# Softmax-free linear attention over 16 images: denominators by column halves, one reciprocal a group, and other orders in the last batch

## The chip, the cores and the metric

The kernel runs on one core of a Trainium2 chip. The metric is the device time of one execution in microseconds (us), lower is better. A core has TensorE (PE, its weight loads shown apart as PEld), VectorE (DVE), ScalarE (ACT), GpSimd (POOL) and SyncE (SP, which here issues every DMA). Each engine works through its own instructions in order; semaphores tie the engines together. A difference of about 0.2% is what a measurement of this kernel can tell from no change.

## What is computed

For each of 16 images x[b] of 256 channels by 6400 tokens (80 by 80), the layer normalises in groups of 8 channels, makes q, k and v, and forms linear attention with 8 heads of 32 channels:

```
xt = gn(x).reshape(B, C, N).transpose(0, 2, 1)
q, k, v = split(xt @ qkv_w.T + qkv_b)            # N = 6400, C = 256
q = relu(q);  k = relu(k + pos_enc)
z = 1 / (einsum('bic,bc->bi', q, k.sum(axis=1)) + 1e-6)   # per head and token
kv = einsum('bjc,bjd->bcd', k, v)                # 32 x 32 per head
out = einsum('bic,bcd,bi->bid', q, kv, z)
y = x + (out @ proj_w.T + proj_b).transpose(0, 2, 1)
```

The change touches z, the reciprocals of the denominators, and how the last image is finished. Everything is float32 at the edges.

## The kernel before

**Tiles.** An image is 13 blocks of tokens: t = 0 to 11 of 512 tokens and t = 12 (LAST) of 256. A block of all 256 channels is a tile of 128 partitions by 2 by 512 (512 KB). B = 16 batches n are one image each, and a batch has 13 steps, one for each block.

**The pipeline.** At step t of batch n, TensorE transposes block t, makes its keys (L603), adds them to the Gram matrix (L615, L617), makes queries for block t-2 (L627), and makes the output of block t-3 of the batch before (L663, 12 matmuls for a block of 512). The Gram matrix and the key sum of batch n-1 are complete only when batch n starts, so the small work that closes batch n-1 lies in the first steps of batch n. We call it the junction: key sums, `key_scale`, `kv_product`, the denominators of group 0 (blocks 0 to 7) at the end of step 0, `m_product` at step 1, and the denominators of group 1 (blocks 8 to 12) at step 2.

**Denominators** (L648). The stationary operand is a window of 32 columns of `swin`, in which the key sums of one half of the channels stand in the columns of four heads and the rest is zero. Each matmul writes 32 partitions of one PSUM bank; four matmuls with j = 0 to 3 write the four strips of 32 partitions. In a strip, half the 32 rows (16 of them) are used, and each row holds 512 tokens. ScalarE adds 1e-6 and copies the bank to `zt` (`z_plus`, L1154). VectorE inverts it in two instructions of 256 columns (`invert`, L937), for group 0 both at step 1, for group 1 one at step 3 and one at step 4. SyncE writes it to HBM (`store_z`, L415, and four small ones for the tail, L420) and then reads it back for each block, copied to the 32 partitions of each head (`load_zb`, L433). GpSimd multiplies q by it (`scale`, L1338).

**Who waits for whom.** In each step VectorE's `key_low` (L885) follows the `invert` of step 1; ScalarE's `key_keep` (L1119) waits for `key_low`, and `normalise` (L1090) stands behind it; SyncE's next load of `xa` (L348) waits for `normalise`, and `store_z` stands behind that load in SyncE's queue. GpSimd takes `scale`, `key_sum` (L1315), `xn_low` (L1301) and `u_low` (L1342) in this order, and TensorE's next key matmuls (L603) need `xn_low`.

**The end** (`finish`, from step 12 of batch 15 on). There is no next batch to work beside, so the outputs of blocks 9 to 12 of batch 14 and of all 13 blocks of batch 15 stand in a row on TensorE. For each block of batch 15, SyncE loads z (`load_z_last`, L433), GpSimd multiplies (`scale_last`, L1331), ScalarE copies twice (`u_last`, L1250 and L1261), VectorE subtracts (`u_low`, L998), TensorE makes the output, and VectorE adds x to it (`residual`, L899). The x of the last batch is loaded once more (`load_last`, L359) into seven places for 512 tokens, used in turn: blocks 4 to 6 wait for a store of batch 14, and blocks 7 to 11 wait for the store of block t-7 of batch 15 (`y_last`). All of it goes through SyncE's one queue.

The order on each engine is the order in which the functions below issue it; nothing reorders it.

## Time and profile before

| | us |
|---|---|
| median of 3 runs | 2628.76 |
| lowest, highest | 2627.99, 2630.11 |
| the profiled execution, its own time | 2629.6 |
| its span, first to last instruction | 2627.5 |
| TensorE busy in it | 2568.3 |
| granted TensorE clock, mean | 0.999 |

The span and what lies around it (2.1 us) make up the profiled execution's time. TensorE is busy for 98% of the span, so its idle stretches, the stretch before it starts and the one after it ends are where time can be won or lost; busy time of another engine counts only where TensorE or the last store waits for it.

### The profile page before, as it was taken

What the parts mean: (1) busy time and instruction counts of PE and PEld (TensorE: products, weight loads), DVE (VectorE), ACT (ScalarE), POOL (GpSimd) and SP (SyncE); (2) the same over time, 40 slices, a digit from 0 to 9 for tenths busy, and PEclk for the clock granted to TensorE, in tenths of its full rate; (3) what the DMA queues carried; (4) which work ended last, traced back from release to release, by engine and by line L of the source; (5) the groups of instructions that cost most, each with busy time, mean ns of one, the idle gap of its engine ahead of it and who ended that gap; (6) DMA issues with size and microseconds to landing.
All of it is one profiled execution on the core that took longest, in us unless ns stands there. A gap on an engine that the chain in (4) does not pass through costs nothing.

```text
span 2627.5 us, 45059 instructions
## 1 busy us (share of the span) xinstructions
PE 2568.3 (98%) x15940; PEld 2203.1 (84%) x15940; DVE 1515.9 (58%) x2405; ACT 1698.8 (65%) x2705; POOL 1979.7 (75%) x1234
## 2 busy tenths in 40 slices
PE   4999999999999999999999999999999999999998
PEld 3878888888888888888888888888888888888886
DVE  5656555565555556555555555656555555554547
ACT  4766766666666666766667666666666666666654
POOL 4958778687787778868687786887768778687875
PEclk9999999999999999999999999999999999999999
DMA  7547867677776867767777677786867677676658
GB/s 257 191 159 254 271 223 264 233 259 254 239 268 225 274 227 260 260 238 256 234 268 261 225 262 251 248 272 222 264 236 263 234 255 258 234 247 205 229 197 300
DMA packets 324189, 642.15 MB, mean 244 GB/s; under 512 B 25728, under 2 KB 47104, under 8 KB 323968
## 3 DMA queue, kind: packets, MB, share of 16 engines
q1 hardware_dynamic: 323968, 639.28, 72.6%
q8 instruction: 130, 2.13, 0.3%
q14 instruction: 91, 0.75, 0.1%
HBM read 519.25 MB, written 119.93 MB: 243 GB/s over the span
## 4 chain that ended last, share of the span: by engine, by line
PE 91%; issue 2%; DVE 2%; POOL 2%; DMA 2%; ACT 1%; SPq 0%; DVEq 0%; ACTq 0%; POOLq 0%
PE banks L603 21%; PE banks L627 20%; PE banks L663 19%; PE banks L615 13%; PE banks L617 7%; PE banks L594 6%; PE banks L648 3%; DMA q<-in_x 1%; PE banks L678 1%; DVE zt L937 1%; POOL hl L1301 0%; POOL kacc L1315 0%; DMA y<-xr 0%; PE banks L685 0%; POOL posb L1326 0%
## 5 line engine op out<-in xcount | busy, mean ns | idle before, releaser
L1315 POOL TENSOR_TENSOR kacc<-kacc,kt 128x512 f32<-128x512 f32 x368 | 477.7, 1298 | 277.3 <-ACT kt L1119 275.5
L1301 POOL TENSOR_TENSOR hl<-xn,hl 128x512 fp32r<-128x512 f32 x384 | 488.9, 1296 | 217.6 <-ACT hl L1102 217.5
L603 PE MATMUL banks<-wqk,hl 128*128 128x256 f32 x4608 | 645.0, 289 | 7.3 <-POOL hl L1301 7.3
L869 DVE TENSOR_TENSOR xt<-banks,xt 128x512 fp32r<-128x512 f32 x400 | 274.9, 687 | 590.0 <-ACT xt L1107 589.7
L627 PE MATMUL banks<-hl,wqk 128*128 128x512 f32 x2304 | 600.0, 396 | 0.2 <-ACT zt L1154 0.2
L615 PE MATMUL banks<-kk,xt 128*128 128x512 f32 x1600 | 583.8, 399 | 3.3 <-DVE kk L885 3.3
L603 PEld LDWEIGHTS banks<-wqk,hl 128*128 128x128 f32 x4608 | 575.0, 191 | 9.1 <-POOL hl L1301 9.1
L663 PE MATMUL banks<-uhl,mhl 128*128 128x512 f32 (+1 forms) x2316 | 541.8, 383 | 2.1 <-DVE xr L899 2.1
L663 PEld LDWEIGHTS banks<-uhl,mhl 128*128 128x128 f32 x2316 | 423.6, 188 | 89.9 <-issue 2.5
L1338 POOL TENSOR_TENSOR q<-q,zb 128x1024 f32<-128x1024 f32 x180 | 433.8, 2410 | 74.5 <-DMA zb<-z_rows 74.4
L627 PEld LDWEIGHTS banks<-hl,wqk 128*128 128x128 f32 x2304 | 406.7, 188 | 92.0 <-issue 1.3
L1112 ACT ACTIVATE kk<-banks 128x512 fp32r<-128x512 f32 x400 | 238.9, 597 | 357.8 <-DVE banks L880 356.0
L617 PE MATMUL banks<-kk,xt 128*128 128x256 f32 x1600 | 449.2, 281 | 0.0
L1342 POOL TENSOR_TENSOR uhl<-q,uhl 128x1024 fp32r<-128x1024 f32 x178 | 427.4, 2401 | 7.2 <-ACT uhl L1136 7.2
L899 DVE SCALAR_TENSOR_TENSOR xr<-banks,biases,xr 128x512 f32<-128x512 f32 x368 | 274.3, 750 | 249.7 <-PE banks L663 247.9
L885 DVE SCALAR_TENSOR_TENSOR kk<-banks,kk 128x512 fp32r<-128x512 f32 x400 | 273.5, 684 | 190.1 <-ACT kk L1112 187.7
L1119 ACT ACTIVATE kt<-banks 128x512 f32<-128x512 f32 x400 | 238.6, 596 | 222.7 <-DVE kk L885 222.6
L1131 ACT ACTIVATE q<-banks,biases 128x512 f32<-128x512 f32 x382 | 262.1, 686 | 147.0 <-PE banks L627 145.3
L615 PEld LDWEIGHTS banks<-kk,xt 128*128 128x128 f32 x1600 | 302.2, 189 | 60.0 <-issue 4.0
L617 PEld LDWEIGHTS banks<-kk,xt 128*128 128x128 f32 x1600 | 303.4, 190 | 0.0
L880 DVE TENSOR_TENSOR banks<-banks,posb 128x512 f32<-128x512 f32 x400 | 276.3, 691 | 12.4 <-PE banks L603 11.4
L1090 ACT ACTIVATE xn<-xa,nbias,rstd 128x512 f32<-128x512 f32 x360 | 272.9, 811 | 0.0
(120 smaller groups left out, 2341.5 us busy)
## 6 DMA issues: line engine op xcount, KB each, us to landing
posb<-pos_plus_bk SPq DMA_DIRECT2D x375, 256.0 KB, 5.0
xs<-in_x SPq DMA_DIRECT2D x184, 512.0 KB, 6.9
xa<-in_x SPq DMA_DIRECT2D x184, 512.0 KB, 6.0
xr<-in_x SPq DMA_DIRECT2D x184, 512.0 KB, 3.9
zb<-z_rows SPq DMA_DIRECT2D x184, 512.0 KB, 6.0
y<-xr SPq DMA_DIRECT2D x184, 512.0 KB, 7.0
z_rows<-zt SPq DMA_DIRECT2D x32, 256.0 KB, 5.5
xr<-in_pos SPq DMA_DIRECT2D x25, 256.0 KB, 4.7
```

Source lines behind the costliest of these rows:

```text
L603: last = mm(psK[:, par(n, h), i * C:(i + 1) * C], hl_of(t)[:, a, c, s:s + P], wqk[:, w, c, C:2 * C], start=(j == 0), stop=(j == len(terms) ...
L615: mm(psG[:, c, :], xt[:, hp, 0, i, c * P:(c + 1) * P], kk[:, hp, i, :, :], start=(h == 0 and i == 0), stop=False)
L617: last = mm(psG[:, c, C:2 * C], xt[:, hp, 1, i, c * P:(c + 1) * P], kk[:, hp, i, 0, :], start=False, stop=(h == NHB - 1 and i == TILES - 1))
L627: last = mm(dst, wqk[:, w, c, m * P:(m + 1) * P], hl_of(t)[:, a, c, :], start=(j == 0), stop=(j == len(terms) - 1))
L663: last = mm(dst, mw[:, w, c, m * P:(m + 1) * P], u[:, a, c, 0:k], start=(j == 0), stop=(j == len(terms) - 1))
L869: v.tensor_tensor(xt[:, hp, 1, :, :].rearrange("p i n -> p (i n)"), psT, xt[:, hp, 0, :, :].rearrange("p i n -> p (i n)"), ALU.subtract).t ...
L880: v.tensor_tensor(psK[:, par(n, h), :], psK[:, par(n, h), :], posb[:, s, :], ALU.add).then_inc(kt_ready, 1)
L899: v.scalar_tensor_tensor(out=xs_, in0=src, scalar=pb[:, m:m + 1], in1=xs_, op0=ALU.add, op1=ALU.add).then_inc(out_ready, 1)
L1301: g.tensor_tensor(hl_of(t)[:, 1, :, s], xn_of(n, t)[:, :, s], hl_of(t)[:, 0, :, s], ALU.subtract).then_inc(xl_ready, 1)
L1315: g.tensor_tensor(both, both, kt[:, par(n, h), :], ALU.add).then_inc(ks_done, 1)
L1338: g.tensor_tensor(q_of(n, t), q_of(n, t), zb_of(t), ALU.mult).then_inc(u_ready, 1)
L1342: g.tensor_tensor(u[:, 1, :, 0:size(t)], q_of(n, t), u[:, 0, :, 0:size(t)], ALU.subtract).then_inc(ul_ready, 1)
```

## The change

The denominators are laid out in another way. Each matmul of 512 columns becomes two of 256, for the first and the second half f of the block, written to neighbouring rows; all 32 rows of a strip are then used, and the bank is 256 columns wide instead of 512. `zt`, the rows in HBM, the copy on ScalarE and the reciprocal shrink to 256 columns with them, and one reciprocal stands for two. For the tail block (f = 0 alone) the four matmuls of 64 columns for each half of the channels stay, now all writing columns 0 to 63 of their strips. Group 1 is inverted at step 3 as a whole; in batch 1 (n == 1) the reciprocal of group 0 moves behind `key_low`.

In `finish`, x of the last batch gets a place of its own for each block (free slots of `q` among them), so blocks 4, 5 and 9 to 11 wait for a `u_low` and blocks 6 to 8 for a store of batch 14, none for a store of its own batch. SyncE's queue is put in another order, `u_low(0)` goes ahead of `m_low` on VectorE, the left-over copies of batch 14 go earlier on ScalarE and GpSimd, and `m_total` leaves its sum in the PSUM bank instead of `mt`; the second `u_last` therefore waits for `ml_ready`.

```diff
@@ constants and buffers @@
-WIN = 12
+WIN = 20
-        zt = sb("zt", [P, 2, BLK])
+        zt = sb("zt", [P, 2, HALF])
-        zd = nc.dram_tensor("z_rows", (2, P, BLK), F32, kind="Internal").ap()
+        zd = nc.dram_tensor("z_rows", (2, P, HALF), F32, kind="Internal").ap()
@@ last_of, load_last @@
-            return (xs[:, 0], xs[:, 1], xa[:, 0], xa[:, 1], xr[:, 0], xr[:, 1], xr[:, 2])[t % 7]
+            return (xs[:, 0], xs[:, 1], xa[:, 0], xa[:, 1], q_of(B - 2, LAST - 2), q_of(B - 2, LAST - 1),
+                    xr[:, 0], xr[:, 1], xr[:, 2], q_of(B - 1, 0), q_of(B - 1, 1), q_of(B - 1, 2))[t]
-                s = last_slot(t)
-                if t in (4, 5, 6):
-                    sp.wait_ge(y_stored[t - 4], landed3(B - 2, t + 5))
-                elif 7 <= t < LAST:
-                    sp.wait_ge(y_last[s], last_no(t) - 16)
-                sp.dma_start(last_of(t), x_part(B - 1, t)).then_inc(x_last[s], 16)
+                if t in (4, 5):
+                    sp.wait_ge(ul_ready, blk_no(B - 2, t + 6))
+                elif t in (6, 7, 8):
+                    sp.wait_ge(y_stored[t - 6], landed3(B - 2, t + 3))
+                elif t in (9, 10, 11):
+                    sp.wait_ge(ul_ready, blk_no(B - 1, t - 9))
+                sp.dma_start(last_of(t), x_part(B - 1, t)).then_inc(x_last[t], 16)
@@ denominators (tensor) @@
-                        w = WIN - 8 * s - c
-                        for j in range(4):
-                            t = 8 * g + 4 * s + j
-                            if g == 1 and s == 1:
-
-                                cols = slice(j * HALF // 4, (j + 1) * HALF // 4)
-                                data = q_of(n, LAST)[:, c, cols]
-                            else:
-                                cols = slice(0, BLK)
-                                data = q_of(n, t)[:, c, :]
-                            last = mm(bank[32 * j:32 * j + 32, cols], swin[:, c, w:w + 32], data,
-                                      start=(s == 0 and c == 0), stop=(s == 1 and c == CC - 1))
+                        for f in range(2):
+
+                            w = WIN - 16 * s - 2 * c - f
+                            for j in range(4):
+                                t = 8 * g + 4 * s + j
+                                if g == 1 and s == 1:
+
+                                    if f == 1:
+                                        continue
+                                    k = HALF // 4
+                                    cols, data = slice(0, k), q_of(n, LAST)[:, c, j * k:(j + 1) * k]
+                                else:
+                                    cols, data = slice(0, HALF), q_of(n, t)[:, c, f * HALF:(f + 1) * HALF]
+                                last = mm(bank[32 * j:32 * j + 32, cols], swin[:, c, w:w + 32], data,
+                                          start=(s == 0 and c == 0 and f == 0), stop=(s == 1 and c == CC - 1 and f == 1 - g))
@@ invert, step, finish (vector) @@
-            def invert(n, g, parts=(0, 1)):
+            def invert(n, g):
                 dve.wait_ge(zt_ready, 2 * n + g + 1)
-                for i in parts:
-                    v.reciprocal(zt[:, g, i * HALF:(i + 1) * HALF], zt[:, g, i * HALF:(i + 1) * HALF]).then_inc(rc_ready, 1)
+                v.reciprocal(zt[:, g, :], zt[:, g, :]).then_inc(rc_ready, 1)
-                if t == 1 and junction:
+                if t == 1 and n > 1:
                     invert(n - 1, 0)
+                if t == 1 and n == 1:
+
+                    invert(n - 1, 0)
-                if t in (3, 4) and junction:
-                    invert(n - 1, 1, (t - 3,))
+                if t == 3 and junction:
+                    invert(n - 1, 1)
@@ z_plus, finish (scalar) @@
-                a(zt[:, g, :], bank, ACT.Identity, bias=zeps).then_inc(zt_ready, 1)
+                if g == 1:
+                    wait(act, z_tail_stored, 64 * n)
+                a(zt[:, g, :], bank[:, 0:HALF], ACT.Identity, bias=zeps).then_inc(zt_ready, 1)
-                        act.wait_ge(m_sum, n)
+                        act.wait_ge(ml_ready, n)
+                u_left(q2, hl[:, 0], q_done, two_no(n - 1, 8, 1))
                 save_q(n - 1, q2, 1, 0)
                 save_q(n - 1, q1, 0, 2)
+                u_left(q1, hl[:, 1], q_done, two_no(n - 1, 9, 1))
                 z_plus(n - 1, 0, psK[:, 0, :])
-                u_left(q2, hl[:, 0], q_done, two_no(n - 1, 8, 1))
-                u_left(q1, hl[:, 1], q_done, two_no(n - 1, 9, 1))
+                u_left(q0, uhl, o_done, two_no(n - 2, q2 - 1, 1))
                 z_plus(n - 1, 1, psK[:, 1, :])
-                u_left(q0, uhl, o_done, two_no(n - 2, q2 - 1, 1))
+                u_last(0)
                 m_high_last()
-                for t in range(NBLK):
+                for t in range(1, NBLK):
@@ end (gpsimd) @@
-            for t in (LAST - 1, LAST):
-                scale(B - 2, t)
-            for t, u in ((LAST - 2, hl[:, 0]), (LAST - 1, hl[:, 1]), (LAST, uhl)):
-                u_low(B - 2, t, u)
+            scale(B - 2, LAST - 1)
+            u_low(B - 2, LAST - 2, hl[:, 0])
+            scale(B - 2, LAST)
+            u_low(B - 2, LAST - 1, hl[:, 1])
+            u_low(B - 2, LAST, uhl)
```

What this makes of the queues at the three places in question is shown below, as the programs issue it. Line numbers of the changed program are one to five off.

VectorE at the junction of batch 1, step 1: `x_low_t` (xt), `key_add` (banks), the reciprocals of group 0 (zt), `key_low` (kk). Before:

```order
L880 TENSOR_TENSOR banks<-banks,posb 128x512 [waits k_done,pos_landed0]
L937 RECIPROCAL zt<-zt 128x256 [waits zt_ready]
L937 RECIPROCAL zt<-zt 128x256
L885 SCALAR_TENSOR_TENSOR kk<-banks,kk 128x2x256 [waits kh_ready]
L869 TENSOR_TENSOR xt<-banks,xt 128x512 [waits xth_ready]
```

Changed:

```order
L881 TENSOR_TENSOR banks<-banks,posb 128x512 [waits k_done,pos_landed0]
L886 SCALAR_TENSOR_TENSOR kk<-banks,kk 128x2x256 [waits kh_ready]
L937 RECIPROCAL zt<-zt 128x256 [waits zt_ready]
L870 TENSOR_TENSOR xt<-banks,xt 128x512 [waits xth_ready]
L881 TENSOR_TENSOR banks<-banks,posb 128x512 [waits k_done,pos_landed1]
```

One reciprocal is gone and the other has moved behind `key_low`; in batches 2 to 15 one is gone and the other keeps its place.

VectorE in `finish`, from the second reciprocal on; `mt` or `banks` at L925 and L926 is `m_total`, `hl_tail` is `m_low`, `hl` is `u_low(0)`, `xr` and `xr_tail` are the residuals of batch 14. Before:

```order
L937 RECIPROCAL zt<-zt 128x256 [waits zt_ready]
L899 SCALAR_TENSOR_TENSOR xr<-banks,biases,xr 128x512 [waits o_done,xr_landed1]
L899 SCALAR_TENSOR_TENSOR xr<-banks,biases,xr 128x512 [waits o_done]
L925 SCALAR_TENSOR_TENSOR mt<-bpb,ksc,banks 128x256 [waits m_done]
L925 SCALAR_TENSOR_TENSOR mt<-bpb,ksc,banks 128x256
L937 RECIPROCAL zt<-zt 128x256 [waits zt_ready]
L932 TENSOR_TENSOR hl_tail<-mt,hl_tail 128x512 [waits mh_ready]
L899 SCALAR_TENSOR_TENSOR xr<-banks,biases,xr 128x512 [waits o_done,xr_landed2]
L899 SCALAR_TENSOR_TENSOR xr<-banks,biases,xr 128x512 [waits o_done]
L998 TENSOR_TENSOR hl<-banks,hl 128x1024 [waits uh_ready]
```

Changed:

```order
L937 RECIPROCAL zt<-zt 128x256 [waits zt_ready]
L900 SCALAR_TENSOR_TENSOR xr<-banks,biases,xr 128x512 [waits o_done,xr_landed1]
L900 SCALAR_TENSOR_TENSOR xr<-banks,biases,xr 128x512 [waits o_done]
L926 SCALAR_TENSOR_TENSOR banks<-bpb,ksc,banks 128x256 [waits m_done]
L926 SCALAR_TENSOR_TENSOR banks<-bpb,ksc,banks 128x256
L1001 TENSOR_TENSOR hl<-banks,hl 128x1024 [waits uh_ready]
L933 TENSOR_TENSOR hl_tail<-banks,hl_tail 128x512 [waits mh_ready]
L900 SCALAR_TENSOR_TENSOR xr<-banks,biases,xr 128x512 [waits o_done,xr_landed2]
```

The last reciprocal is gone, and `u_low(0)` now stands ahead of `m_low` and of the residual of block 11.

SyncE in `finish`, from the last z load of the first five on; `xn`, `kt` and `zb` are the places of z, `xr` and `q` from `in_x` are x of the last batch, `y` is a store. Before:

```order
L374 DMA y<-xr 128x2x512 [waits out_ready]
L359 DMA xr<-in_x 128x2x512 [waits y_stored0]
L374 DMA y<-xr 128x2x512 [waits out_ready]
L415 DMA z_rows<-zt 128x512 [waits zb_tail_landed,rc_ready,zb_landed1,zb_landed0]
L420 DMA z_tail_rows<-zt 8x64 x4
L433 DMA xn<-z_rows 128x1x1024 [waits z_stored0,u_ready]
L374 DMA y<-xr 128x2x512 [waits out_ready]
L359 DMA xr<-in_x 128x2x512 [waits y_stored1]
L433 DMA xn<-z_rows 128x1x1024 [waits z_stored0,u_ready]
L374 DMA y<-xr_tail 128x2x256 [waits out_ready]
L433 DMA kt<-z_rows 128x1x1024 [waits z_stored0,u_ready]
```

Changed:

```order
L355 DMA q<-in_x 128x2x512 [waits ul_ready]
L370 DMA y<-xr 128x2x512 [waits out_ready]
L411 DMA z_rows<-zt 128x256 [waits zb_tail_landed,rc_ready,zb_landed1,zb_landed0]
L416 DMA z_tail_rows<-zt 16x64 x4
L355 DMA xr<-in_x 128x2x512 [waits y_stored0]
L370 DMA y<-xr 128x2x512 [waits out_ready]
L429 DMA xn<-z_rows 128x1x1024 [waits z_stored0,u_ready]
L355 DMA q<-in_x 128x2x512 [waits ul_ready]
L429 DMA xn<-z_rows 128x1x1024 [waits z_stored0,u_ready]
L370 DMA y<-xr 128x2x512 [waits out_ready]
L355 DMA xr<-in_x 128x2x512 [waits y_stored1]
L355 DMA q<-in_x 128x2x512 [waits ul_ready]
```

The store of group 1's rows has moved ahead of the first load that waits for a store of y. The z of block 7 (`kt`) still stands behind the second such load; two x loads into `q` have come between.

## Rows read from the trace of the kernel before

**Rows 1.** The page, part 1: busy us, share of the span, instructions.

```profile
PE 2568.3 (98%) x15940; PEld 2203.1 (84%) x15940; DVE 1515.9 (58%) x2405; ACT 1698.8 (65%) x2705; POOL 1979.7 (75%) x1234
```

**Rows 2.** Waits: engine, line, released by: us in total, times, longest us.

```profile
PE banks L603 <- POOL hl L1301: 7.3, 7, 2.0
```

**Rows 3.** Groups of instructions by form: shapes, count, busy us, mean ns.

```profile
L648 PE MATMUL banks<-q,swin 128*32 128x512 f32 x764 | 89.0, 596 | 0.0
...
L648 PE MATMUL banks<-q_tail,swin 128*32 128x64 f32 x256 | 6.5, 219 | 0.0
...
L937 DVE RECIPROCAL zt<-zt 128x256 f32<-128x256 f32 x64 | 109.4, 1730 | 6.6 <-ACT zt L1154 6.6
```

**Rows 4.** Timeline, PE: start us, us, line, count; denominators of one junction.

```profile
1128.49 3.64 PE L648 MATMUL banks<-q,swin 128*32 128x512 f32 x32
...
1156.38 0.41 PE L648 MATMUL banks<-q_tail,swin 128*32 128x64 f32 x16
```

**Rows 5.** Timeline, junction of batch 1, PE and DVE; brackets: idle before, its releaser.

```profile
180.07 0.47 PE L615 MATMUL banks<-kk,xt 128*128 128x512 f32 x1 [0.76 <-DVE kk L885]
...
184.53 0.63 PE L594 MATMUL banks<-ident,xn 128*128 128x128 f32 x4 [1.22 <-DVE xt L869]
...
176.03 3.35 DVE L937 RECIPROCAL zt<-zt 128x256 f32<-128x256 f32 x2
```

**Rows 6.** Chain that ended last: denominators of group 0 in three batches, start us, us.

```profile
1929.47 3.57 PE banks L648 x32
...
2089.34 3.57 PE banks L648 x32
...
2250.59 3.57 PE banks L648 x32
```

**Rows 7.** Timeline, POOL at two junctions, and SP at the second of them.

```profile
1473.47 2.40 POOL L1338 TENSOR_TENSOR q<-q,zb 128x1024 f32<-128x1024 f32 x1 [4.69 <-DMA zb<-z_rows]
...
2114.36 2.39 POOL L1338 TENSOR_TENSOR q<-q,zb 128x1024 f32<-128x1024 f32 x1 [6.27 <-DMA zb<-z_rows]
...
2103.14 0.40 SPq L415 DMA_DIRECT2D z_rows<-zt  x1
2108.45 0.52 SPq L433 DMA_DIRECT2D zb<-z_rows  x1
```

**Rows 8.** Timeline, PE at the end: outputs of blocks 11, 12, then batch 15.

```profile
2580.30 1.67 PE L663 MATMUL banks<-uhl,mhl 128*128 128x256 f32 x12 [2.12 <-DVE xr L899]
2582.00 5.74 PE L663 MATMUL banks<-hl,hl_tail 128*128 128x512 f32 x24
...
2601.53 3.00 PE L663 MATMUL banks<-uhl,hl_tail 128*128 128x512 f32 x12 [1.86 <-DVE xr L899]
...
2616.09 4.31 PE L663 MATMUL banks<-hl,hl_tail 128*128 128x512 f32 x24
```

**Rows 9.** Timeline, DVE: the last two residuals.

```profile
2620.05 1.41 DVE L899 SCALAR_TENSOR_TENSOR xr<-banks,biases,xr 128x512 f32<-128x512 f32 x2 [1.16 <-DMA xr<-in_x]
2621.38 0.86 DVE L899 SCALAR_TENSOR_TENSOR xs_tail<-banks,biases,xs_tail 128x256 f32<-128x256 f32 x2
```

**Rows 10.** Timeline, SP at the end: issues of stores and loads.

```profile
2567.11 0.34 SPq L415 DMA_DIRECT2D z_rows<-zt  x1
2569.24 1.17 SPq L433 DMA_DIRECT2D xn<-z_rows  x2
...
2572.40 0.62 SPq L374 DMA_DIRECT2D y<-xr  x1
2580.59 0.38 SPq L359 DMA_DIRECT2D xr<-in_x  x1
...
2584.84 0.52 SPq L433 DMA_DIRECT2D xn<-z_rows  x1
```

**Rows 11.** Windows: us, busy of PE, PEld, DVE, ACT, POOL, PEclk, DMA share, GB/s.

```profile
2560.00:2565.00 5.00, 5.00 (x40) 2.59 (x33) 1.34 (x1) 1.28 (x3) 0.75 (x1) 1.00 0.02 5
...
2605.00:2610.00 5.00, 4.97 (x22) 3.76 (x21) 3.92 (x6) 3.54 (x4) 4.14 (x2) 1.00 1.05 402
```

62 lines of the change are left out of this document (30 added, 32 removed).

## Prediction, made before the changed kernel ran

> **What bounds the kernel now.** I read the page's busy shares first. TensorE is busy for 98% of the span [rows 1], at the full granted clock; VectorE, for which most of this change is written, for 58%. So VectorE's saving cannot be the answer by itself: 32 reciprocals of 1.73 us [rows 3] are 55 us of VectorE, and what they are worth is what TensorE waits for behind them. Second, the waits of TensorE. Apart from the start, which the change leaves alone, they are few: seven waits for `xn_low` with 7.3 us in sum [rows 2], about half of it in the start, and some at the junction of batch 1 and after batch 15's last key block. Third, the timelines at those places, which give three stretches where TensorE or the last store is held up by something that this change touches. They are the three terms below. Everywhere else TensorE works through an unchanged list without a gap, 159.87 us from one junction's denominators to the next [rows 6].
>
> **The denominators on TensorE: 0.** Group 0 had 16 matmuls, each recorded twice, 32 records in 3.64 us [rows 4]. Now it has 32 matmuls of half the columns. Four strips run at once, and a set of four records of 512 columns takes (3.64 - 0.60) / 7 = 0.43 us, start to start. Halving the columns gives 0.21 us for twice as many sets: 15 x 0.217 + 0.38 = 3.64 us again, where 0.38 is a record of 256 columns by the line through 0.596 us at 512 and 0.219 us at 64 [rows 3]. The risk is a cost for each record that doesn't shrink. The records of 64 columns bound it: 16 of them take 0.41 us, so they start (0.41 - 0.22) / 15 = 13 ns apart [rows 4], and a record of 256 columns has 53 ns to hide such a step. I take 0. The upper bound is the part of a record that doesn't depend on its columns, 0.219 - 64 x 0.84 ns = 0.165 us, paid once more by each added set: 8 sets in group 0 and 4 in group 1, 12 x 16 batches x 0.165 = 32 us. The tail's matmuls keep count and size. A lower bound under zero has no source, since the columns streamed are the same.
>
> The Trainium skill, page TensorEngine Tiling (Array Packing), section Instruction Overhead, speaks against this split: each matmul carries about 60 cycles of overhead, so that very short ones cost as much as ones of 60 columns. At 2.4 GHz that would be an estimated 25 ns for each of the 768 added records, 19 us, and 2639 us in all. The trace's 13 ns between records of 64 columns doesn't agree with it where four strips run side by side.
>
> **ScalarE, DMA, GpSimd in the junctions: 0.** `z_plus` and the row stores get shorter, the reads for each block keep their 4 KB runs, and one more wait (`z_tail_stored`) is for stores of a batch ago. The SyncE queue keeps its order there.
>
> **Term 1, junction of batch 1: 2.0 us.** The two reciprocals take 3.35 us from 176.03, `key_low` stands behind them, and TensorE waits 0.76 us for it at 180.07. ScalarE's `normalise` and the next transposed copy are late for the same reason, and TensorE waits another 1.22 us at 184.53 [rows 5]. With `key_low` first, it comes 3.3 us earlier, and the single reciprocal of 1.73 us fits before VectorE's next work. Both waits go: 0.76 + 1.22 = 2.0. Next late is the `key_low` of step 2 behind statistics, a wait that exists now and stays. Bounds 0.8 (only the first goes) and 2.2.
>
> **Term 2, late z rows in three batches: 3.9 us.** In each junction SyncE issues the store of the rows (2103.14) only after an `xa` load that waits for `normalise`, which waits for `key_low`, which waits for the reciprocals. The read goes out at 2108.45 and GpSimd waits for it, with `xn_low` queued behind [rows 7]. In twelve of the fifteen junctions it waits 4.69 us at most and TensorE notices nothing. In three the read lands late, GpSimd waits over 6 us, 6.27 at the most, and the batch takes longer: 2089.34 to 2250.59 is 161.25 us against 159.87 [rows 6], 1.38 more. The other two give slightly less; I take 3.9 for the three. One reciprocal fewer makes `key_low`, the `xa` load and the row store 1.6 us earlier, so the wait of 6.27 becomes 4.7, in the class that costs nothing. I take all 3.9. Bounds: 0, if the landings get later by as much as the issues get earlier, and 4.1, since no other batch has anything to give. Group 1 has the same gain, a step earlier, and nobody waits there.
>
> **Term 3, the end: 3.5 us** (bounds 0 and 6.0), in three pieces.
>
> First, when the first output of batch 15 starts (2582.00 [rows 8]). One reciprocal of group 0 less lets the row store go at 2565.2 instead of 2567.11, and the first z reads at 2567.3 instead of 2569.24 [rows 10]. GpSimd, which had three `u_low` left, now has only that of block 12, which waits for TensorE's block 9 and is done before the read lands. So it scales block 0 from about 2571.5 to 2574, ScalarE copies twice (2 us), VectorE has `u_low(0)` at 2577.5, then `m_low` and the residual of block 11, for which TensorE waits 2.12 us now. That output starts near 2579, and block 0 at 2580.8: gain 1.2. Here a danger lies: `u_low(0)` now stands ahead of `m_low` and of the residual, so a z read that lands late delays TensorE's block 11/12 hand-over too. Bounds 0 and 1.4.
>
> Second, the run of 13 outputs. It takes from 2582.00 to 2620.40 = 38.4 us; 24 records take 5.74 us, so a block takes (5.74 - 0.40) / 23 x 12 = 2.78 us, and 12 blocks and a tail of half the columns 34.7. The 3.7 between are mostly waits for blocks whose z came late, 1.86 of them before 2601.53 [rows 8]. The z of block 5 was issued at 2584.84, behind the store of group 1's rows and an x load that waited for a store of y until 2580.59 [rows 10]. Now the row store goes out at 2574, ahead of that wait. The wait itself stays: the store it waits for goes out at about 2571 instead of 2572.40, with one more x load ahead of it, and lands near 2580. So z of block 5 is issued at 2581, of block 6 at 2582, in time. But the next x load waits for the store of block 10, issued at 2580.3, until 2588.3 (8 us, as 2572.40 to 2580.59 [rows 10]), and z of block 7 stands behind it, at 2589.5. It lands about 7 us later, and 6 us more of GpSimd, ScalarE and VectorE give 2602.6, where TensorE could take it at 2600.3. That gives 2.3 back. Gain 1.4; bounds -1 and 3.7.
>
> Third, the last residuals. VectorE waits 1.16 us for x of block 11, which pushes the tail's from 2620.4 to 2621.4 [rows 9]. With a place for every block, x is there: gain 0.9, bounds 0 and 0.9. The store of the last tile and its 5.2 us to the end stay.
>
> DMA is the cover for all of this. Its share is 0.02 in 2560 to 2565 and 1.05 from 2605 to 2610 [rows 11]. The bytes stay (but for 0.25 MB of rows), two x loads move into the idle time, and so the queue of transfers ends earlier; but in the middle it stays full.
>
> **Sum.** 2.0 + 3.9 + 3.5 = 9.4 us off the profiled execution's own 2629.6 gives 2620.2. That execution lies 0.8 us above the median of 2628.76; how many late landings the other runs had isn't shown, and since the forecast has none, I don't lower it: 2620.
>
> **Rivals.** (a) *The z rows stay late.* The read is issued 1.6 us earlier but lands in another mix of loads. Against it: the waits fall into those up to 4.69 and those over 6, nothing between. Then term 2 is zero: 2624.1. Chance 0.13. (b) *The end gives nothing.* The x loads wait for stores of batch 14 still, everything after is behind them, and the transfer queues are full there. Terms 1 and 2 alone: 2623.7. Chance 0.12. (c) *The end is free.* No late z at all, 6.0 instead of 3.5: 2617.7. Chance 0.09. (d) *The split matmuls cost TensorE time*, at each junction, on the engine that sets the pace. Between 13 ns for each of 768 added records (10 us) and 0.165 us for each added set (32 us) it gives 2630 to 2652; it decides from 9.4 us, that is 12 ns a record. For it: the smallest spacing seen is about that. Against it: that spacing is an eighth of the 107 ns between records of 512 columns, just as the columns are, so nothing in it is fixed. Chance 0.05, of which 0.04 end slower by more than 0.2%.
>
> **How the numbers follow.** The forecast has 0.59 and by itself the range 2617 to 2623. What is left over, 0.02, is slower by a mishap at the end. A difference of 0.2% (5.3 us) is about what a measurement of this kernel can tell from no change: faster is under 2623.5. The forecast and (c) give 0.68, half of (b) and a fifth of (a) add 0.09: 0.77. Within 0.2% is the rest of these and 0.01 of (d): 0.17. Slower 0.06. The range, 2616 to 2624.5, takes in (a), (b) and (c) and leaves out (d).
>
> **What would show it.** Right: denominators of group 0 again about 3.64 us for 64 records; no wait at 180 and 184; GpSimd's wait at the junctions 3 to 4.7 us and all batches 159.9 us apart; block 0's output near 2574.9 (2580.8 less the 5.9 of terms 1 and 2), one wait of some 2 us before block 7, and no wait of VectorE for x. Wrong: groups of denominators longer by 0.4 us or more, waits of over 6 us at junctions, or an end that is as long as now from block 0's output on (from 2582.00 to the span's 2627.5 now 45.5 us; forecast 2624.0 - 2580.8 = 43.2).

## The result and the profile after

| | before, us | changed, us |
|---|---|---|
| median | 2628.76 | 2620.66 |
| lowest, highest of 7 executions each | 2625.24, 2630.11 | 2618.88, 2622.67 |
| the profiled execution, its own time | 2629.6 | 2620.28 |
| its span | 2627.5 | 2618.5 |

The ratio of changed to before is 0.9971 [0.996, 0.9983]. Measured again beside other kernels it was 0.9974 [0.9964, 0.9984], with a median of 2621.09. The forecast was 2620.0, range 2616 to 2624.5. So the total came out as forecast, but two pieces of its third term did not: the run of outputs at the end got longer instead of shorter, and the last stores won more than they were given.

The page of the changed kernel, part 1, answers to [rows 1]:

```profile
PE 2569.6 (98%) x16708; PEld 2229.5 (85%) x16708; DVE 1470.2 (56%) x2373; ACT 1691.9 (65%) x2705; POOL 1979.4 (76%) x1234
```

VectorE lost 45.7 us of busy time and TensorE gained 1.3, yet the time fell by 8.1. Neither number is the answer; it lies where TensorE stood still. The groups by form, columns as in [rows 3]:

```profile
L649 PE MATMUL banks<-q,swin 128*32 128x256 f32 x1528 | 89.5, 381 | 0.0
...
L937 DVE RECIPROCAL zt<-zt 128x256 f32<-128x256 f32 x32 | 55.8, 1743 | 6.3 <-ACT zt L1158 6.3
```

Twice the records with half the columns have nearly the busy time of before (89.5 against 89.0), and 32 reciprocals are left of 64. The timeline of the junction of batch 1, TensorE and VectorE, against [rows 4, 5]:

```profile
169.73 3.66 PE L649 MATMUL banks<-q,swin 128*32 128x256 f32 x64
...
189.90 0.47 PE L614 MATMUL banks<-kk,xt 128*128 128x512 f32 x1 [0.56 <-DVE kk L886]
...
177.55 1.74 DVE L937 RECIPROCAL zt<-zt 128x256 f32<-128x256 f32 x1
```

The group of denominators takes 3.66 us, 0.02 more than before. The waits of 0.76 and 1.22 us are gone; the wait of 0.56 us at step 2 is the only bracket that TensorE shows between the two groups of denominators.

**Where the 9.0 us of span went.** The starts of group 0's denominators, read in both timelines, cut the span into the same stretches:

| stretch, us | before | changed | gain |
|---|---|---|---|
| start to the denominators of junction 1 | 169.66 | 169.73 | -0.07 |
| junction 1 to junction 2 | 159.50 | 157.15 | 2.35 |
| junctions 2 to 15, 13 batches | 2082.48 | 2078.78 | 3.70 |
| junction 15 to `finish` | 147.59 | 147.64 | -0.05 |
| denominators of `finish` to the end of the span | 68.27 | 65.20 | 3.07 |

In the third row all 13 batches of the changed kernel take 159.90 or 159.91 us. Before, nine took 159.86 or 159.87, one 160.07, and three 161.24, 161.26 and 161.11, of which the second is the one in [rows 6, 7]. GpSimd's waits for the rows of denominators in junctions 2 to 15, a line of the view of waits (in total, times, longest us), before and after:

```profile
POOL q L1338 <- DMA zb<-z_rows: 71.0, 18, 6.3
```

```profile
POOL q L1343 <- DMA zb<-z_rows: 66.8, 21, 5.4
```

The end of the changed kernel, timeline of TensorE, against [rows 8]; the first line is the output of block 12 of batch 14, then come blocks of batch 15:

```profile
2573.00 1.67 PE L664 MATMUL banks<-uhl,mhl 128*128 128x256 f32 x12 [0.68 <-DVE xr L900]
2574.51 5.63 PE L664 MATMUL banks<-hl,hl_tail 128*128 128x512 f32 x24
...
2591.94 2.98 PE L664 MATMUL banks<-uhl,hl_tail 128*128 128x512 f32 x12 [0.65 <-DVE q L900]
2597.16 7.32 PE L664 MATMUL banks<-hl,hl_tail 128*128 128x512 f32 x24 [2.23 <-DVE q L900]
2604.99 2.98 PE L664 MATMUL banks<-xt,hl_tail 128*128 128x512 f32 x12 [0.52 <-DVE xr L900]
...
2610.53 4.31 PE L664 MATMUL banks<-hl,hl_tail 128*128 128x512 f32 x24
```

The wait of 2.12 us ahead of block 12's output is 0.68 us now. The run of 13 outputs goes from 2574.51 to 2614.84: 40.3 us, where it took 38.4. It waits 0.65, 2.23 and 0.52 us, and the group at 2597.16 (blocks 7 and 8) takes 7.32 us instead of some 5.6, as at 2604.37 in the trace of before. The windows of that stretch (us, busy TensorE, granted clock, DMA share, GB/s) show the clock:

```profile
2590.00:2595.00 5.00, 4.28 (x18) 1.00 1.05 408
2595.00:2600.00 5.00, 2.84 (x10) 0.85 1.03 406
2600.00:2605.00 5.00, 4.48 (x17) 0.80 1.05 404
2605.00:2610.00 5.00, 5.00 (x22) 1.00 0.96 373
```

The chain of work that ended last says what the end hangs on (start us, us):

```profile
2577.92 7.43 DMA xn<-z_rows
...
2585.43 2.37 POOL q L1336
2587.80 10.65 DMA zb<-z_rows
...
2598.51 2.38 POOL q L1336
...
2604.11 0.75 DVE xr L900
...
2604.99 9.87 PE banks L664 x48
```

The matmuls are not on it from 2577.92 to 2604.99. The reads of the rows for block 6 and, above all, for block 9 are; that for block 9 was issued at 2587.80, landed at 2598.45, and GpSimd took it up at 2598.51. SyncE had issued those for blocks 5 and 7 at 2575.92 and 2581.48, GpSimd could use them at 2581.78 and 2590.68. SyncE's last lines and VectorE's last line, against [rows 9]; the first line is the last store of before:

```profile
2622.27 0.37 SPq L363 DMA_DIRECT2D y<-xs_tail  x1
```

```profile
2610.55 4.05 SPq L359 DMA_DIRECT2D y<-q  x3
2615.86 0.37 SPq L359 DMA_DIRECT2D y<-xs_tail  x1
...
2614.95 0.88 DVE L900 SCALAR_TENSOR_TENSOR xs_tail<-banks,biases,xs_tail 128x256 f32<-128x256 f32 x2 [0.75 <-PE banks L664]
```

From TensorE's end to the span's end it takes 3.7 us where it took 7.1: VectorE waits for no x, and the last store is done 2.6 us behind its issue instead of 5.2.

### The profile page after: what moved, and what is told of

Read it like the earlier page. It is cut to its first block, busy times and chain, and to the rows that moved or that the text cites. A ratio compares the mean times of both kernels' runs of the same rounds, so it can differ in the third digit from the quotient of the medians.

```text
span 2618.5 us, 46565 instructions
## 1 busy us (share of the span) xinstructions
PE 2569.6 (98%) x16708; PEld 2229.5 (85%) x16708; DVE 1470.2 (56%) x2373; ACT 1691.9 (65%) x2705; POOL 1979.4 (76%) x1234
## 3 DMA queue, kind: packets, MB, share of 16 engines
q8 instruction: 136, 2.23, 0.3%
## 4 chain that ended last, share of the span: by engine, by line
PE 95%; DMA 1%; POOL 1%; ACT 1%; issue 1%; DVE 1%; SPq 0%; DVEq 0%; ACTq 0%; POOLq 0%
PE banks L602 21%; PE banks L626 21%; PE banks L664 20%; PE banks L614 14%; PE banks L616 7%; PE banks L593 7%; PE banks L649 3%; DMA q<-in_x 1%; PE banks L679 1%; PE banks L686 0%; DMA zb<-z_rows 0%; POOL posb L1331 0%; DMA xn<-z_rows 0%; POOL hl L1306 0%; PE banks L671 0%
## 5 line engine op out<-in xcount | busy, mean ns | idle before, releaser
L900 DVE SCALAR_TENSOR_TENSOR xr<-banks,biases,xr 128x512 f32<-128x512 f32 x366 | 274.2, 750 | 298.0 <-PE banks L664 297.5
```

Of the source, the lines that this page charges most:

```text
L900: v.scalar_tensor_tensor(out=xs_, in0=src, scalar=pb[:, m:m + 1], in1=xs_, op0=ALU.add, op1=ALU.add).then_inc(out_ready, 1)
```

## Experiments

The kernel before was run beside each set; its median was 2628.1 to 2628.7. The times are medians.

**Both halves of the change apart.** First the denominators and junctions alone, with the end's orders as before; in `finish` the rest of the change is undone:

```diff
-                    xr[:, 0], xr[:, 1], xr[:, 2], q_of(B - 1, 0), q_of(B - 1, 1), q_of(B - 1, 2))[t]
+            return (xs[:, 0], xs[:, 1], xa[:, 0], xa[:, 1], xr[:, 0], xr[:, 1], xr[:, 2])[t % 7]
... (places of x, SyncE's order)
-                m_total(n - 1, psT, in_bank(psT))
-                u_low(n - 1, 0)
-                m_low(n - 1, in_bank(psT))
+                m_total(n - 1, psT, mt)
+                m_low(n - 1, mt[:])
... (the other orders in `finish`)
```

> The new layout of the denominators and the single reciprocals, with the end of the kernel before (places of x, SyncE's order, VectorE's, ScalarE's and GpSimd's orders in the end). The theory (the junctions give 5.9 us, the end's other orders give 3.1 by themselves) expects about 2622.9 against 2628.8, no TensorE wait at the junctions of batches 2 to 15, and an end as long as before or shorter by up to 1.9 us, since one reciprocal less there lets the first z reads go earlier. The rival that the two parts need each other (a shorter junction gives nothing unless the end is reordered) expects under 3 us of gain.

Then the end alone, with matmuls of 512 columns and two reciprocals a group:

```diff
-                        for f in range(2):
-                            w = WIN - 16 * s - 2 * c - f
+                        w = WIN - 8 * s - c
...
-                if t == 3 and junction:
-                    invert(n - 1, 1)
+                if t in (3, 4) and junction:
+                    invert(n - 1, 1, (t - 3,))
```

> The changed end alone, with the denominators of the kernel before (512 columns, two reciprocals for each group, in the end one behind the other). The theory expects 1 to 3 us of gain, 2626 to 2628, with the last residuals free of waits for x and the time from TensorE's last output to the end short (about 3.7 us instead of 7.1), but a run of 13 outputs that is no shorter than 38.4 us. The rival that the end's gain comes from the earlier z reads (one reciprocal less) expects no gain here or a loss.

Measured: 2622.31 (0.9978 [0.9969, 0.9987]) for the first, 2627.76 (0.9996 [0.9987, 1.0005]) for the second. The first kernel's stretches are those of the changed kernel up to `finish` (157.15, 2078.78), and its end takes 66.9 us. The second's junctions are those of before (159.48 for batch 1, two late landings), and its end takes 70.7. So the denominators bring 5.8 us by themselves, and the new end orders 0.4 by themselves, which the interval does not tell from nothing, but 1.2 to 1.7 on top of the others. The time of the second kernel lies in the range of the theory, but its run of outputs takes 44.3 us. Two waits in it show why:

```profile
2596.25 4.58 PE L662 MATMUL banks<-hl,hl_tail 128*128 128x512 f32 x12 [2.06 <-DVE xa L898]
...
2613.24 4.58 PE L662 MATMUL banks<-xt,hl_tail 128*128 128x512 f32 x12 [2.75 <-DVE xr L898]
```

These are the outputs of blocks 5 and 9, each 1.6 us longer than the 2.98 of a free one, at a lower granted clock. (This execution took 2630.16, 2.4 us above the median, so others of this kernel may have had less of it.) SyncE stands at a load that waits for a store of batch 14 until 2582.60 there, and the reads of rows for the later blocks follow behind it and the loads of x.

The first kernel's run of outputs takes 37.0 us (2575.88 to 2612.92), with 1.5 us of lower clock in its first group, where the changed kernel takes 40.3. So in these two traces the old order of the end is 3.3 us better in the run, and the new one wins 1.4 at the start of the first output and 3.6 behind the last. The first kernel's last two stores of y:

```profile
2614.06 0.37 SPq L363 DMA_DIRECT2D y<-xr  x1
2614.84 0.37 SPq L363 DMA_DIRECT2D y<-xs_tail  x1
```

Its span ends at 2620.2, 5.4 us behind the last issue. In both kernels with the new end the same store takes 2.6 us. So the short last store comes with the new end. The likely reason is its places for x: no load waits for a store of the last batch any more, and the transfers have thinned out by then (DMA share 0.64 in 2610 to 2615, against 1.05 with the old orders). No run changes the places alone.

**The place of the reciprocal in batch 1.** The reciprocal goes ahead of `key_low` again:

```diff
-                if t == 1 and n > 1:
+                if t == 1 and junction:
                     invert(n - 1, 0)
-                if t == 1 and n == 1:
-
-                    invert(n - 1, 0)
```

> The changed kernel with the reciprocal of group 0 in batch 1 put back ahead of the low half of the keys. If the move gave the 2.4 us of batch 1's junction, TensorE waits there again and the time is 0.5 to 2 us longer than the changed kernel's. If the shorter reciprocal alone gave it, TensorE's waits at about 180 and 184 us stay away and the time is the same within 0.3 us. By the trace of before the second: the first wait was 0.76 us behind 3.35 us of reciprocals, and 1.6 of these are gone.

Measured: 2622.11 (0.9979 [0.997, 0.9988]). TensorE at that junction:

```profile
183.91 0.63 PE L593 MATMUL banks<-ident,xn 128*128 128x128 f32 x4 [0.62 <-DVE xt L870]
```

The wait of 0.76 us is gone all the same, and that of 1.22 has become 0.62. The batch takes 157.72 us. So of term 1's 2.35 us, 1.78 belong to the shorter reciprocal and 0.57 to its new place. Neither theory was quite right: one wait is gone, half of the other is still there. The median lies 1.0 to 1.5 us above the changed kernel's, of which 0.57 is explained; in this trace 1.1 more went in two later batches (160.70 and 160.21 us) that the edit doesn't touch.

**SyncE's order at the end.** The reads of rows for blocks 5 to 8 go ahead of the load of x for block 6, that for block 9 ahead of those for blocks 7, 8 and 11, and during the last stores the reads go ten blocks ahead instead of nine:

```diff
-            load_last(6)
-            store_y(B - 2, LAST - 2)
             load_z_last(5)
-            load_last(9)
+            store_y(B - 2, LAST - 2)
             load_z_last(6)
-            store_y(B - 2, LAST - 1)
-            load_last(7)
-            load_last(10)
+            load_last(9)
             load_z_last(7)
-            store_y(B - 2, LAST)
+            store_y(B - 2, LAST - 1)
             load_z_last(8)
...
-                if t + 9 < NBLK:
-                    load_z_last(t + 9)
+                if t + 10 < NBLK:
+                    load_z_last(t + 10)
```

> The changed kernel with another order in SyncE's queue at the end: the z reads of blocks 5 to 9 go ahead of the x loads of blocks 6 to 8 and 11, of which the first waits for a store of y from 2570.6 to 2574.9 with everything behind it. The theory that the 5.6 us by which the run of 13 outputs is longer than its work (40.3 against 34.7) come from z reads that land 6 to 11 us after their issue, late in a full queue, expects three of the four waits of TensorE in that run to go, the granted clock to stay at 1.00 there, and a gain of 2 to 5 us on the changed kernel, 2616 to 2618.5. The rival that the queue of transfers is full anyway, whatever goes first, expects the same time within 1 us, with VectorE waiting for x in place of z.

Measured: **2615.64** (0.9955 [0.9942, 0.9967]), 5 us below the changed kernel. The reads for blocks 5 to 9 go out at 2571.06, 2572.32, 2574.00, 2575.69 and 2578.01, with no wait of SyncE for a store of y among them. They don't land faster (5.4, 6.7, 8.0, 8.9 and 11.1 us behind their issue, in the changed kernel 5.8, 7.4, 9.1, 9.5 and 10.6), but they are issued 4.9 to 9.8 us earlier. TensorE has one wait left in the run, which takes 35.0 us:

```profile
2574.63 5.63 PE L665 MATMUL banks<-hl,hl_tail 128*128 128x512 f32 x24
...
2602.53 2.97 PE L665 MATMUL banks<-kk,hl_tail 128*128 128x512 f32 x12 [0.52 <-DVE xr L901]
```

**The same order with the denominators of before.** The edit is that of the last kernel, made in the end-only one:

```diff
-            load_last(6)
-            store_y(B - 2, LAST - 2)
             load_z_last(5)
-            load_last(9)
+            store_y(B - 2, LAST - 2)
```

> The denominators and junctions of the kernel before, the changed end, and in it SyncE's order that gave 2615.6 us with the changed denominators (the reads of the rows for blocks 5 to 9 ahead of the loads of x, and always ten blocks ahead). Theory: the order's gain of 5.0 us belongs to the end alone: 2627.8 less 5.0 is 2622.8 (2621.5 to 2624.5), with the run of 13 outputs within 36 us instead of 39 and waits of VectorE of 1 us or more for x at most at one block. Rival: the order helps only where the rows are stored as early as the shorter reciprocals let them be; then waits of 1 to 2 us stay ahead of block 12 and of block 0, and the time is 2625.5 or more.

Measured: 2621.79 (0.9975 [0.9964, 0.9985]), 6.0 us below the end-only kernel. The theory holds: the order's gain belongs to the end alone (5.0 with the new denominators, 6.0 with the old). Its run takes 35.5 us.

**Transfers of x taken away.** Eight loads of x shrink from 512 columns to 8:

```diff
-                sp.dma_start(last_of(t), x_part(B - 1, t)).then_inc(x_last[t], 16)
+                part = x_part(B - 1, t) if t < 4 or t == LAST else x_part(B - 1, t)[:, :, 0:8]
+                dst = last_of(t) if t < 4 or t == LAST else last_of(t)[:, :, 0:8]
+                sp.dma_start(dst, part).then_inc(x_last[t], 16)
```

> The changed kernel with the second load of x for blocks 4 to 11 of the last batch cut to 8 of 512 columns (the output of those blocks is left wrong in the rest): eight transfers of 512 KB leave the queues, no instruction goes and no order changes. Theory: the rows for blocks 5 to 9 land 5.9 to 10.7 us behind their issue because they share the queues with these loads; without them they land within 4.5 us, the run of 13 outputs takes 34.7 to 35.5 us instead of 40.3, and the time is 2615 to 2616.5. Rival: SyncE issues them too late, since it stands 4.3 us at the store of y ahead of them; then the wait ahead of block 7 stays above 1.5 us, the run takes 37 us or more, and the time is 2617.5 or more.

Measured: 2614.66 (0.9947 [0.9933, 0.996]). The wait ahead of block 7 is gone with SyncE's order untouched, and the run takes 34.3 us (2575.00 to 2609.26). The reads for blocks 5 to 9 land 4.2, 6.1, 6.5, 6.1 and 5.8 us behind their issue: more than the 4.5 expected, but for block 9 4.8 less than in the changed kernel. SyncE also issues that one 2.4 us earlier (2585.39), since the load of x ahead of it, which waits for a store, goes out 2.3 us earlier. So the reads were late because they shared the transfers with x, mostly in landing and partly in being issued. The kernel with the reads first, which moves every byte, comes within 1.0 us of this time.

**VectorE's order in the run:**

```diff
-                    if t + 2 < NBLK:
-                        u_low(n - 1, t + 2)
                     residual(n - 1, t, psX[:, 0:2] if t % 2 else psG)
+                    if t + 2 < NBLK:
+                        u_low(n - 1, t + 2)
```

> The changed kernel with one swap in VectorE's order at the end: the residual of block t stands ahead of the low part of the queries of block t+2. Theory: the waits of TensorE ahead of block 7 (2.23 us, ended by VectorE's residual of block 5) are at bottom waits for the rows of block 7, which land 9.2 us behind their issue; then the swap only turns the releaser into the low part itself, the wait stays 1.5 to 2.5 us and the time is 2620 to 2622. Rival: it is the coupling in VectorE's order that costs, since the bank of block 5 is held back by a product for block 7; then the waits of the run fall below 1 us in all and the time is 2617.5 to 2618.8.

Measured: 2620.79 (0.9971 [0.996, 0.9982]), the time of the changed kernel. TensorE there:

```profile
2597.61 7.36 PE L664 MATMUL banks<-hl,hl_tail 128*128 128x512 f32 x24 [2.54 <-DVE hl L1001]
```

The wait stays, and only its releaser is another: `u_low` instead of the residual. The "<-DVE q L900" of the changed kernel was a wait for rows from HBM, passed on by three engines.

**What became of the late landings.** Every reciprocal twice, first into a scratch tile:

```diff
+                v.reciprocal(zscr[:, g, :], zt[:, g, :])
                 v.reciprocal(zt[:, g, :], zt[:, g, :]).then_inc(rc_ready, 1)
```

> The changed kernel with every reciprocal done twice: first into a scratch tile that nobody reads, then as before, so that VectorE spends 3.5 us a group again instead of 1.74 us. Theory: the three late landings of the kernel before (GpSimd waits of 6.14 to 6.27 us, batches of 161.1 to 161.3 us) went because the shorter reciprocal lets the rows of denominators be stored 1.6 us earlier. Then the row store is issued some 13.9 us behind the start of the group of denominators instead of 12.3, landings near 5.9 us come back at one to three junctions, and the time is 2622 to 2625.5. Rival: VectorE's part has nothing to do with it (the landings were late by chance, or went for the smaller transfer itself); then the batches stay at 159.90 to 159.95 us with GpSimd waits below 5.5 us, and the time is 2620.5 to 2621.5. In either case batch 1 may lose up to 0.6 us, where the reciprocal stands ahead of the outputs' residual.

Measured: 2633.26 (1.0021 [1.0011, 1.0031]), 7.8 us above the range of the theory and 11.8 above the rival's. Most batches take 160.31 us, 0.40 more. Of the 12.3 us that this profiled execution is longer than that of the changed kernel, the 13 batches have 7.2, batch 1 has 2.0, and the last batch and the end 3.0. At the start of group 0 nothing is lost. The loss stands behind group 1, whose two reciprocals now follow each other, where the kernel before put them in steps 3 and 4 (VectorE, then TensorE):

```profile
365.54 1.74 DVE L938 RECIPROCAL zscr<-zt 128x256 f32<-128x256 f32 x1
367.20 1.69 DVE L939 RECIPROCAL zt<-zt 128x256 f32<-128x256 f32 x1
368.81 0.63 DVE L871 TENSOR_TENSOR xt<-banks,xt 128x512 fp32r<-128x512 f32 x1
...
367.95 1.57 PE L627 MATMUL banks<-hl,wqk 128*128 128x512 f32 x6
369.58 0.63 PE L594 MATMUL banks<-ident,xn 128*128 128x128 f32 x4
```

`x_low` comes 1.6 us later and frees the bank of the transposes later; the next ones start 1.63 us behind the queries, not 1.41, and the other 0.2 us is lost right after. That is under the size at which the view prints a wait, and it comes in every batch. The experiment was thus no test of the landings, so the next one doubles group 0 alone, in batches 2 to 15:

```diff
+                if g == 0 and 1 <= n < B - 1:
+                    v.reciprocal(zscr[:, g, :], zt[:, g, :])
                 v.reciprocal(zt[:, g, :], zt[:, g, :]).then_inc(rc_ready, 1)
```

> The changed kernel with one more reciprocal into a scratch tile ahead of the real one for the first group alone, in batches 2 to 15 (batch 1, the last batch and all second groups as changed), so that the rows are stored at 13.9 us behind the start of the group again and nothing else moves. Theory: a later store brings the late landings back in some executions; the median is then 2622 to 2624.5, the executions spread over 3 us or more, and a profiled one may or may not show GpSimd waits of 6 us. Rival: the moment of the store has nothing to do with them; the median stays within 0.7 us of the changed kernel run beside it, as does the spread.

Measured: 2621.61 (0.9976 [0.9966, 0.9986]), against 2621.09 for the changed kernel beside it. By the medians the rival is right, within 0.7 us. By the trace one late landing is back:

```profile
991.75 2.40 POOL L1346 TENSOR_TENSOR q<-q,zb 128x1024 f32<-128x1024 f32 x1 [5.99 <-DMA zb<-z_rows]
```

That batch takes 161.02 us. All traces together say more, and what they say is about the moment, not the length, of GpSimd's wait. Five have the row store 13.9 us behind the denominators' start; their longest waits are 6.3, 6.1, 6.0, 5.1 and 5.1 us. Eight have it at 12.3 us; their longest are 5.8, 5.5, 5.4, 5.4, 5.3, 5.0, 5.0 and 4.8. Here are the longest of the eight and another one of this kernel:

```profile
1149.91 2.41 POOL L1345 TENSOR_TENSOR q<-q,zb 128x1024 f32<-128x1024 f32 x1 [5.78 <-DMA zb<-z_rows]
```

```profile
830.70 2.40 POOL L1346 TENSOR_TENSOR q<-q,zb 128x1024 f32<-128x1024 f32 x1 [5.32 <-DMA zb<-z_rows]
```

The wait of 5.78 us (the kernel with small loads of x) cost its batch nothing, the one of 5.32 cost 0.46. Count from the start of group 0's denominators: the first ends at 23.00 us, the second at 24.15. In the seven batches of all traces that lost time to late rows, the loss is the moment at which GpSimd takes the rows, less 23.7 us: 24.15 cost 0.46, 24.68 cost 0.99, 24.83 cost 1.12, 24.96 cost 1.24, 25.08 cost 1.37. With the shorter reciprocal GpSimd begins to wait at 17.2 us instead of 18.8, because the keys come earlier for it too (`key_sum` starts at 9.45 us instead of 11.05). So the wait stays about as long (median 4.1 us in the changed kernel, 4.0 in this one, 4.7 before), and all of it lies 1.6 us earlier; in the eight traces no rows are taken later than 23.00. One read in them landed late (5.27 us from issue to use, where most take 3.5 to 4.3) and was taken at 22.50, at no cost.

Over the usual batch, four of the five traces (without the doubled kernel) lost 4.2, 2.4, 1.6 and 0.2 us. Without the 0.2 that three of them lose in batch 9, where the rows are not the cause (the doubled kernel loses it too, with rows taken at 22.85), that is 1.9 on the mean by late rows; the eight lost nothing by them (0.3 on the mean elsewhere). So the earlier store is worth about 1.9 us on the mean of these traces, less than the 3.7 between the two profiled executions. Moving the takes of the eight 1.6 us later, an estimate by the same line, would cost them 0.5 us on the mean, and the medians of the last experiment give 0.5 too (the two medians' executions spread over 3 us each). Its size stays open between these.

**The clock behind the long wait.** Six useless matmuls just ahead of it; block 6's second half is computed twice:

```diff
+                    if (n, t, m) == (B - 1, 6, 1):
+                        for j, (c, w, a) in enumerate(terms):
+                            mm(dst, mw[:, w, c, m * P:(m + 1) * P], u[:, a, c, 0:k],
+                               start=(j == 0), stop=(j == len(terms) - 1))
```

> The changed kernel with six useless matmuls: the second half of block 6's output in the last batch is computed twice (the second chain overwrites the first), 1.4 us of work for TensorE just ahead of its wait for block 7. Theory: the slow group behind that wait (24 matmuls in 7.32 us instead of 5.60, granted clock 0.85 and 0.80) comes from the 2.2 us in which TensorE stands still; with 0.9 us of waiting left the clock stays at 1.00, the run of 13 outputs takes 38.5 to 39 us instead of 40.3, and the time is 1.2 to 1.8 us below the changed kernel run beside it, in spite of more work. Rival: the clock falls for another reason (the queues at their full rate), or the drop belongs to single executions; then the time is within 0.6 us of it.

and the changed kernel again:

> The changed kernel once more, unchanged, beside the other two. Both theories expect 2620.7 us (2619.5 to 2622), batches of 159.90 us and a granted clock below 1 behind the wait ahead of block 7; a trace without that drop would say that it belongs to single executions.

Measured: 2621.94 (0.9976 [0.9966, 0.9985]) and 2621.09. The theory falls: more work brought no gain. The median is 0.85 us above the repeat's, a little more than the rival allowed too. With a wait of 0.88 us left the clock did stay at 1.00, but that shows nothing, for in the trace of the unchanged repeat it stays at 1.00 behind 2.74 us. This trace also tells why nothing was gained; TensorE waits once more in it:

```profile
2597.76 5.69 PE L664 MATMUL banks<-hl,hl_tail 128*128 128x512 f32 x24 [2.74 <-DVE q L900]
2604.79 2.97 PE L664 MATMUL banks<-xt,hl_tail 128*128 128x512 f32 x12 [1.34 <-DVE xr L900]
```

Block 9 starts at 2604.79 with the full clock and at 2604.99 with the slow group. It waits for its rows, which GpSimd took up at 2598.26 here and at 2598.51 there. In all seven profiled executions with this order of SyncE and VectorE and full loads of x, block 9 starts 6.5 us behind that moment. The 1.7 us that the lower clock costs came out of a wait of 1.3 to 1.9 us that would have stood there.

## Why the prediction was right, and where it was not

**Denominators on TensorE, 0.** Right in kind: 3.66 us against 3.64. A batch takes 0.04 us more, 0.8 ns for each of its 48 added records, some 0.5 us in all; the term was short by that. The bounds of 13 ns a record and 0.165 us a set were far off. By the rate of the long ones (430 ns for a set of four with 512 columns) a set with 64 columns takes 54 ns and each of its four records 13, so the 13 ns was all columns, not a floor. The rule of the Trainium skill, page TensorEngine Tiling (Array Packing), section Instruction Overhead, that each matmul carries about 60 cycles, would have made it an estimated 19 us, counted for each added record as the prediction did (half of that for each added matmul, since a matmul has two records); the measured 0.5 doesn't agree with it where four strips run side by side.

**Term 1, 2.0.** Measured 2.35, above its bound of 2.2: both waits went, and so did the short one of 0.21 us behind them. 0.57 of it is the new place, the rest the shorter reciprocal, which the working had mixed.

**Term 2, 3.9.** Between the two traces 3.70, or 4.2 less the 0.5 of the denominators. The cause is as forecast, rows stored 1.6 us earlier, and no wait costs anything now. But the step "so the wait of 6.27 becomes 4.7" is not what happens: GpSimd comes 1.6 us earlier too, so the wait keeps about its length (5.4 us at the longest, outside the forecast's 3 to 4.7) and only its end moves ahead of the 23.7 us at which it begins to cost. Nor is it so that "no other batch has anything to give": the batch of 160.07 gave its 0.2 back too, of a cause that stays open. And the step that took the profiled execution as the kernel's state was weak: three late landings in one execution is more than the mean. That also explains why the forecast's 9.4 from 2629.6 was about right while the medians differ by 7.6 to 8.1 only: the profiled execution of before lay 0.8 us above its median, that of the changed kernel 0.4 below.

**Term 3, 3.5.** Measured 3.07, from three pieces of which one is near. *The start of the first output* won 1.56 (forecast 1.2): 21.21 us from the denominators, where it took 22.77. It needs both parts of the change, as the two halves show. *The run of 13 outputs* was to win 1.4 and lost 1.9. The step failed at "That gives 2.3 back". Up to there it came out right, in part by luck: less the 5.9 us that terms 1 and 2 take away, the forecast had the rows of block 7 landing at 2590.6 (GpSimd took them at 2590.68) and TensorE's block 7 at 2596.7 (2597.16). But it had them issued at 2583.6 and landing in 7 us; they were issued at 2581.48 and took 9.1. It saw no wait ahead of block 6 either, which cost 0.65 us. Then it let the rest run free. But the rows of block 9 were issued at 2587.80, behind two more loads of x (blocks 11 and 8) and the first store of the batch, and landed 10.65 us later. They set the rest, whatever TensorE did before. The 7 us for a landing was too little already by the trace of before, where the reads for blocks 6 and 7 took 8.4 and 8.2. *The last residuals* were to win 0.9, and won 3.4. Of this 0.9 is the wait for x. The step that failed is "The store of the last tile and its 5.2 us to the end stay": that time was queueing behind loads and stores, and shrank to 2.6 with the new end, whose loads of x go earlier. Two errors, of -3.3 and +2.5 us, nearly cancelled. The total was right partly by that luck. The last sign, the time from block 0's output to the end of the span, is 44.0 us, between the forecast's 43.2 and the 45.5 of before.

**The rivals.** (a) and (b) didn't come; (c), a free end, wasn't this change, but the kernel with the reads first shows that it was to be had by order alone: 2615.64. (d) was 20 times smaller than its lower price, 0.5 us against 10.

The sentence on DMA, "in the middle it stays full", was the key to the end, and it was not followed through. The Trainium skill, page DMA: Bandwidth & Descriptors, section Queues, rings and completion order, says that each DMA engine takes the descriptors of a ring in ring order; it does not promise that they are completed in that order. In the changed kernel's trace the reads for blocks 5 to 9 did land in order of issue (2581.7, 2585.3, 2590.6, 2592.5, 2598.4), and an earlier place among the same transfers brought 5 us. By that rule the reads to move were those that an engine waits for soonest.

## What to carry to other kernels

When all loads and stores of an ending go through one full queue, its order is a schedule: put the transfer that the critical engine needs next ahead of larger ones that are needed later, and ahead of any wait of the issuing engine. Follow each late read to its engine, not only the first one, because behind a repaired or predicted wait the next landing sets the time. Take a rare wait's cost from several traces: one execution may show three of them, another none. And judge a late transfer by the moment at which the engine takes it, counted from the critical engine's work, not by the length of the wait, which grows when the waiting engine comes earlier.

## What the hardware showed that was not expected

- Behind waits of TensorE of 1.90, 2.06, 2.23, 2.25, 2.54 and 2.75 us at the end the next group ran 1.5 to 1.8 us longer with a granted clock of 0.66 to 0.89 in the windows around it, a mix of 2.4 and 1.2 GHz. Behind others of 1.86, 1.92, 1.94, 2.12, 2.21, 2.74 and 2.89 us it stayed at 1.00. The same program showed both, so the wait's length alone doesn't decide.
- Splitting a matmul of 512 columns in two of 256, four strips side by side, costs 0.8 ns per added record.
- The first read of rows (0.5 MB) in a junction took 3.5 to 4.3 us from issue to use in most batches of all traces and up to 5.9 in a few; reads of the same size at the end of the changed kernel landed after 7.4, 9.1, 9.5 and 10.6 us, where the DMA share was 1.03 to 1.05.
- A loss of 0.40 us in each of 13 batches, in pieces of 0.2 us that the list of waits doesn't show, added up to 5 us in the kernel with doubled reciprocals. Batch periods show such a loss, the waits don't.
